# Expert weights loaded four to a DMA instead of two, and earlier in the order of SyncE's queue

## The chip, the cores and the metric

The kernel runs on one core of a Trainium2 chip. The metric is the device time of one execution in microseconds (us), smaller being better. Engines: PE (matrix), DVE (vector), ACT (scalar), POOL (GpSimd), SP (SyncE, which here does nothing but issue DMAs and wait).

## What is computed

Two layers on 16 batches of 128 rows of 256 numbers. Each step adds to x a function of its layer norm:

```
x = x + _L0_xattn_ref(_layernorm(x), k, fside, ctx, ctx, 8)     # long convolution
x = x + _L0_ffn_ref(_layernorm(x), ...)                         # router, top 2 of 16, rank 16
x = x + _L1_xattn_ref(_layernorm(x), ctx, wq, bq, wkv, ...)     # 16-head attention, quantized q and out
x = x + _L1_ffn_ref(_layernorm(x), router_w, ..., gate_w, up_w, down_w, shared_...)

# _L1_ffn_ref
scores = jnp.sqrt(jax.nn.softplus(flat @ router_w.T))
_, idx = jax.lax.top_k(scores + expert_bias, 4)
...
for each of 32 experts: acc + p[:, None] * _clamped_swiglu(flat, wg, wu, wd)
out = out + _clamped_swiglu(flat, shared_gate_w, shared_up_w, shared_down_w)
```

The change concerns the weights of the 32 experts of the last step. One expert has 128 x 768 numbers (gate, up and down), 393 KB; all 32 have 12.6 MB.

## The kernel before

The program is one loop over ticks (`for t in range(TICKS)`), written out once for each engine. A step stands in the engine's instructions at the tick that a table gives it: `T_PE`, `T_DVE`, `T_ACT`, `T_POOL`, `T_SP`. A tick is not a time: it only sets the order in which each engine meets its steps. `at(t, first, every, n)` places n of them, `every` ticks apart. Batch b of the first three steps of the layers is placed 128 ticks after batch b-1. From tick `LOOP` = 3122 on the expert tiles follow: 95 tiles of 128 rows, each with the rows of one expert.

Rows reach their experts through memory. For each batch ACT writes the normed rows four times to `xn_rows` (`Xd`, L1159). SP loads 128 of these rows into one of seven buffers `stage` (`row_load`, L1402; 64 loads, j = 4b + k). POOL scatters them by an indirect DMA to their places in `expert_rows` (`Xs`, L1387). Load j waits until scatter j-7 has completed (`d_sc`), since it takes the same buffer; scatter j waits for load j (`d_st`) and for the routing of its group of batches (`ixl`, which DVE makes at L1007). The groups are batches 0 to 3, 4 to 7, 8 to 11, 12 to 13, 14 to 15. After scatter 55, the last of batch 13, SP gathers the rows of the first tiles (L1455, L1471, `work<-expert_rows`), and PE transposes them (L371) and multiplies (L387, L354). The loads of batches 14 and 15 follow behind the twelfth gather.

The weights of the experts lie in `arena`, 768 columns for each. The same columns serve earlier work: those of experts 0 to 19 (`early` = 20) hold `kv`, `z` and `vT` of the convolution, and so SP waits for `s_uT` and `s_swb`; those of 20 to 27 hold `u` and the transposed context `cT`, and so SP waits for `s_vp`, NB of them (the value projection of the last batch, L493 on PE); those of 28 to 31 hold `xT`, `hb`, `wx` and `kz`, and so SP waits for `s_S` (the scores of the last batch, L630). These are the steps "w0" (L1432), "w1" (L1436) and "w2" (L1440) of SP. PE waits for all of them before its first expert matmul (L381). All DMAs that SP issues go to one hardware queue; ACT's go to another, POOL's to a third.

Other steps that the prediction speaks of: POOL's `rsD` (L1302 to L1306, the reciprocal deviation of the last layer norm, one for each batch), ACT's `xnD` (L1115 at this place, the normed rows), PE's `xnTD` (L536, L537, their transposes), `op` (L529, output projection of attention), ACT's "xr" (L1171, loads of rows for the shared expert) with their transposes on PE (L550), and the shared expert's last matmul `dn` (L570).

Of the kernel before, what the change touches and what calls it, by code (L numbers as in the profile page):

```python
# [15 lines left out]
NE = 32  # L16
# [31 lines left out]
NP = NB // 2  # L48
# [20 lines left out]
def at(t, first, every, n):  # L69
    d = t - first  # L70
    return (d // every,) if d >= 0 and d % every == 0 and d // every < n else ()
# [35 lines left out]
def build(nc, a_x, a_ctxT, a_tk, a_pack, a_qp, a_rows, a_w, a_dest, a_pad, out):  # L107
    ctx = ExitStack()
    with ctx:
# [23 lines left out]
        wv_ = arena[:, :].rearrange("p (e n) -> p e n", n=768)  # L133
        work = sb("work", [128, WORK])

        def cutter(base):
# [22 lines left out]
        early = 20  # L159
# [40 lines left out]
        st = {n: sb(f"st{n}", [128, 2, 16]) for n in "ABCD"}  # L200
# [66 lines left out]
        d_w = sem("d_w")  # L267
# [9 lines left out]
        s_wq, s_wqT, s_wint, s_wsc, s_swb = (sem(n) for n in ("s_wq", "s_wqT", "s_wint", "s_wsc", "s_swb"))  # L277
# [41 lines left out]
            "xnC": 878, "q": 923, "PT": 1035}  # L319
        T_POOL = {"rsA": 131, "rsB": 699, "rsC": 827, "rsD": 1170, "vc": 315, "us": 415, "kv": 296, "xb": 818,  # L320
            "xc": 1118, "list": 1926}
        T_SP = {"fill": 1162, "st": 1863, "w0": 2620, "w1": 3043, "w2": 3053}
        TICKS = LOOP + PACE * (NT + 9)

        def when(table, name, g):
# [9 lines left out]
        def tensor_program(pe):  # L335
# [4 lines left out]
            def tile_steps(t):  # L340
                if t < NT:
                    m = int(t >= EARLY)
                    i, w = t - EARLY * m, (NWE, NWL)[m]
                    field = (words[m][i % w] >> 5 * (i // w)) & 31
                    base[t] = [pe.snap(field * 768, min_val=0, max_val=768 * (NE - 1))]
                for n in at(t, 5, 1, NT):
                    p = ybanks[n % 2]
                    if n >= 2:
                        pe.wait_ge(s_y, n - 1)
                    else:  # L350
                        pe.wait_ge(*sbanks.free[n])
                    pe.wait_ge(s_hT, n + 1)
                    for k, e in enumerate(base.pop(n)):
                        i = pe.matmul(p[U * k:U * k + U, 0:256], hT[n % 2][:, U * k:U * k + U],  # L354
                                      arena[:, 512:][:, bass.ds(e, 256)], start=True, stop=True)
                    i.then_inc(s_yp, 1)
                for n in at(t, 0, 1, NT):
                    p = xbanks[n % 2]
                    if n < 2:
                        pe.wait_ge(*(banks.free[3], cbanks.free[0])[n])  # L360
                    if n == 46:
                        pe.wait_ge(s_tm, 1)
                        pe.transpose(p[0:4, 256:384], th4[:, 0:4], ident).then_inc(s_t5, 1)
                    if n == 48:
                        pe.wait_ge(s_tm, 2)
                    if n == 50:
                        pe.transpose(p[0:1, 256:260], th4[0:4, 4:5], ident[0:4, 0:4]).then_inc(s_t5, 1)
                    if n == 52:
                        pe.wait_ge(s_tm, 3)
                    pe.wait_ge(d_g[n % 4], 16 * Q * (n // 4 + 1))  # L370
                    pe.transpose(p[:, 0:128], xg[n % NX][:, 0:128], ident)  # L371
                    pe.transpose(p[:, 128:256], xg[n % NX][:, 128:256], ident).then_inc(s_gP, 1)
                for n in at(t, 4, 1, NT):
                    if n == 0:
                        pe.wait_ge(s_oT, NB)
                    pe.wait_ge(s_h2, n + 1)
                    pe.transpose(po[:, 0:128], th[n % 3][:, 0, :], ident).then_inc(s_hP, 1)  # L377
                for n in at(t, 1, 1, NT):
                    p = gbanks[n % 2]
                    if n == 0:  # L380
                        pe.wait_ge(d_w, 16 * NE // 2)  # L381
                    if n < 2:
                        pe.wait_ge(*banks.free[n])
                    pe.wait_ge(s_gT, n + 1)
                    for c in range(2):
                        for k, e in enumerate(base[n]):
                            i = pe.matmul(p[U * k:U * k + U, 0:256], xgT[n % 3][:, 128 * c + U * k:128 * c + U * k + U],  # L387
                                          arena[:, 256 * c:][:, bass.ds(e, 256)], start=(c == 0), stop=(c == 1))
                    i.then_inc(s_gup, 1)

            pe.wait_ge(d_id, 16)
            for t in range(TICKS):
# [3 lines left out]
                for n in at(t, T_PE["wsc"], 16, 2):  # L396
                    p, free = bk.take(("wint", n), s_wint, n + 1)
# [4 lines left out]
                    for c in range(2):  # L402
                        for k in range(2):
                            o = 256 * k + 128 * c
                            i = pe.transpose(pb[:, o:o + 128], wtb[:, 256 * c + 128 * k:256 * c + 128 * k + 128], idb[:, :])
# [3 lines left out]
                    p, free = bk.take(("swb", n), s_swb, 1)  # L409
                    pe.wait_ge(*free)  # L410
                    pe.wait_ge(s_pconst, 1)
                    for c in range(2):
                        i = pe.matmul(p[:, 128 * c:128 * c + 128], ones[:, :], wdg[:, c, :], start=True, stop=True)
                    i.then_inc(s_wsc, 1)
                for b in at(t, T_PE["xnTA"], 128, NB):
                    p, free = bk.take(("vT", b), s_vT, b + 1)
# [4 lines left out]
                for n in at(t, T_PE["uT"], 128, 2 * NP):  # L421
                    r, co = n // 2, n % 2
                    p, free = bk.take(("xA", n), s_xA, n + 1)
# [3 lines left out]
                    for half in range(2):  # L427
# [3 lines left out]
                        for k in range(8):  # L431
                            i = pe.matmul(pv, zv[:, k, :], ident, is_transpose=True, start=False, stop=(k == 7))  # L432
                    i.then_inc(s_uT, 1)
                for b in per(t, T_PE["xnTB"]):
                    p, free = bk.take(("xT", b), s_xT, b + 1)
# [4 lines left out]
                for b in per(t, T_PE["h"]):  # L440
                    p, free = bk.take(("h", b), s_eh, b + 1)
# [8 lines left out]
                for b in per(t, T_PE["rl"]):  # L450
                    p, free = bk.take(("l", b), s_l, b + 1)
# [136 lines left out]
                for m in (*at(t, T_PE["wordE"], 1, 1), *(1 for _ in at(t, T_PE["word"], 1, 1))):  # L588
                    n = len(words[m])
# [803 lines left out]
        def sync_program(sp):  # L1393
# [30 lines left out]
            for t in range(TICKS):  # L1424
                for e in (*at(t, 0, 1, 14), *(14 + n for n in at(t, T_SP["fill"], 36, NE - 14))):
                    sp.dma_start(Xs[e * NB * 128:(e + 1) * NB * 128, :].rearrange("(j p) d -> p j d", p=128),
                                 stage[:, e % 4, :].unsqueeze(1).broadcast_to((128, NB, ROW))).then_inc(d_zero, 16)
                for i in at(t, T_SP["w0"], 32, early // 2):
                    if i == 0:
                        sp.wait_ge(s_uT, 2 * NP)  # L1430
                        sp.wait_ge(s_swb, 1)
                    sp.dma_start(wv_[:, 2 * i:2 * i + 2, :], a_w[2 * i:2 * i + 2].rearrange("e p n -> p e n")).then_inc(d_w, 16)  # L1432
                for _ in at(t, T_SP["w1"], 1, 1):
                    sp.wait_ge(s_vp, NB)
                    for e0 in range(early, NE - 4, 2):
                        sp.dma_start(wv_[:, e0:e0 + 2, :], a_w[e0:e0 + 2].rearrange("e p n -> p e n")).then_inc(d_w, 16)  # L1436
                for _ in at(t, T_SP["w2"], 1, 1):
                    sp.wait_ge(s_S, 4 * NB)
                    for e0 in range(NE - 4, NE, 2):
                        sp.dma_start(wv_[:, e0:e0 + 2, :], a_w[e0:e0 + 2].rearrange("e p n -> p e n")).then_inc(d_w, 16)  # L1440
                for g in range(NG - 1):
                    for n in at(t, when(T_SP, "st", g), (16, 16, 8, 8)[g], KT * (GROUPS[g][1] - GROUPS[g][0])):
                        row_load(KT * GROUPS[g][0] + n)
# [125 lines left out]
```

## Time and profile before

| | us |
|---|---|
| three runs | 693.38, 694.88, 698.75 (median 694.88) |
| the profiled execution, its own time | 698.75 |
| its span, first to last instruction | 697.0 |
| PE, DVE, ACT, POOL busy in it | 582.6, 449.2, 385.6, 378.5 |

The profile is of one execution, the slowest of the three; its span leaves 1.75 us of its time outside. A busy time is the sum over an engine's instructions, and tells nothing of what waits for what: for that there are the chain that ended last and the timelines.

### The profile page before, as it was taken

The page shows a single profiled execution, that of the slowest core. Times are in us where ns is not written, and L with a number is a line of the kernel's source. Part 1 is how long each engine was busy: PE and PEld are TensorE (multiplying, and loading weights), DVE is VectorE, ACT ScalarE, POOL GpSimd, SP SyncE. Part 2 cuts the span into 40 slices and gives each one's busy share as a digit, 9 for nine tenths or more (in the row PEclk, how much of TensorE's full clock was granted, in tenths as well). Part 3 has the DMA queues.
Part 4 walks back from the last instruction along what each step waited for, and adds up shares of the span by engine and source line. Part 5 has one row for each costly group of instructions (what it writes and reads, how often), then busy time and mean ns, then how long its engine had stood idle before and what let it go on. Part 6 is the DMA issues. An engine that isn't in the chain of part 4 may idle for free.

```text
span 697.0 us, 14316 instructions
## 1 busy us (share of the span) xinstructions
PE 582.6 (84%) x4069; PEld 467.5 (67%) x4069; DVE 449.2 (64%) x1392; ACT 385.6 (55%) x1132; POOL 378.5 (54%) x527
## 2 busy tenths in 40 slices
PE   1588999999989999989898788785779999999920
PEld 0487787887767778867776566563557787787810
DVE  1546656777766876767666666375756777555596
ACT  1002456666777656875567866663535666566610
POOL 6847847357554565586554415424255555555560
PEclk9999999999999999999999979886899999999975
DMA  7989999999999995212334945849544555455689
GB/s 272 246 180 334 335 334 334 334 328 327 318 305 331 317 307 171 72 62 90 120 114 142 352 132 148 264 131 327 164 141 124 167 161 155 152 160 161 206 271 309
DMA packets 135868, 155.02 MB, mean 222 GB/s; under 512 B 15376, under 2 KB 125072, under 8 KB 135536
## 3 DMA queue, kind: packets, MB, share of 16 engines
q1 hardware_dynamic: 117664, 122.50, 59.2%
q0 software_dynamic: 7632, 20.98, 8.4%
q10 hardware_dynamic: 10496, 10.62, 4.9%
q8 instruction: 36, 0.59, 0.4%
q14 instruction: 40, 0.33, 0.2%
HBM read 53.92 MB, written 100.28 MB: 221 GB/s over the span
## 4 chain that ended last, share of the span: by engine, by line
PE 60%; DVE 12%; POOL 8%; issue 7%; DMA 5%; ACT 5%; ACTq 0%; another core or an unknown queue 0%; SPq 0%; DVEq 0%; POOLq 0%
PE ps L387 11%; PE pc L650 10%; PE pS L354 6%; POOL arena L1373 4%; PE pS L630 4%; PE ps L432 3%; PE po L601 2%; DMA work<-y_rows 2%; PE ps L616 2%; PE ps L459 2%; PE ps L493 2%; DMA expert_rows<-stage,ixl 2%; PE ps L476 2%; PE ps L562 1%; PE ps L485 1%
## 5 line engine op out<-in xcount | busy, mean ns | idle before, releaser
L650 PE MATMUL pc<-arena,tk 128*128 128x128 f32 x768 | 109.7, 296 | 13.3 <-POOL arena L1373 7.3
L650 PEld LDWEIGHTS pc<-arena,tk 128*128 128x128 f32 x768 | 97.9, 204 | 25.7 <-issue 13.5
L1373 POOL TENSOR_TENSOR arena<-arena 128x512 f32<-128x512 f32 x64 | 90.5, 1428 | 20.7 <-ACT arena L1178 20.6
L387 PE MATMUL ps<-arena,work 128*128 x380 | 100.0, 386 | 0.6 <-ACT work L1132 0.6
L1387 POOL DMA_INDIRECT expert_rows<-stage,ixl x64 | 64.0, 1000 | 45.4 <-DVE ixl L1007 22.4
L1245 ACT ACTIVATE work<-pS,work 128x128 f32<-128x128 f32 x256 | 72.7, 369 | 4.9 <-DVE work L909 3.7
L706 DVE TENSOR_SCALAR work<-ps 128x256 f32<-128x256 f32 x95 | 40.1, 422 | 49.9 <-PE ps L387 46.4
L387 PEld LDWEIGHTS ps<-arena,work 128*128 128x128 f32 x380 | 66.0, 194 | 6.5 <-issue 1.2
L354 PE MATMUL pS<-arena,tk 128*128 x190 | 60.7, 401 | 4.7 <-ACT tk L1127 3.4
L1122 ACT ACTIVATE tk<-work 128x128 f32<-128x128 f32 x95 | 29.5, 311 | 63.3 <-DVE work L706 52.3
L909 DVE TENSOR_REDUCE work<-pS 128x4 f32<-128x512 f32 x64 | 43.9, 686 | 27.0 <-PE pS L630 25.4
L891 DVE TENSOR_TENSOR arena<-pc,arena 128x512 f32<-128x512 f32 x64 | 43.5, 679 | 17.8 <-PE pc L650 17.7
L1314 POOL DMA_INDIRECT y_rows<-tk,work x38 | 41.3, 1087 | 24.6 <-ACT tk L1137 19.3
L354 PEld LDWEIGHTS pS<-arena,tk 128*128 128x128 f32 x190 | 28.7, 189 | 22.9 <-issue 15.4
L616 PE MATMUL ps<-pk,work 128*128 128x128 f32 x256 | 40.5, 282 | 3.0 <-ACT work L1245 1.8
L1237 ACT ACTIVATE work<-ps 128x512 f32<-128x512 f32 x64 | 37.9, 592 | 3.0 <-PE ps L616 0.8
L630 PE MATMUL pS<-arena,work 32*128 32x256 f32 x256 | 38.1, 417 | 0.8 <-ACT work L1230 0.8
L1302 POOL TENSOR_TENSOR stB<-stB,epsc 128x1 f32<-128x1 f32 x16 | 3.0, 190 | 62.2 <-DVE stB L666 62.0
L1302 POOL TENSOR_TENSOR stD<-stD,epsc 128x1 f32<-128x1 f32 x16 | 3.2, 200 | 60.3 <-DVE stD L666 60.0
L616 PEld LDWEIGHTS ps<-pk,work 128*128 128x128 f32 x256 | 29.7, 143 | 6.8 <-issue 3.3
L432 PE MATMUL ps<-pk,arena 128*128 128x128 f32 x256 | 32.3, 273 | 0.0
L1127 ACT ACTIVATE tk<-po 128x128 f32<-128x128 f32 x95 | 25.9, 272 | 9.7 <-PE po L377 5.8
(286 smaller groups left out, 1444.8 us busy)
## 6 DMA issues: line engine op xcount, KB each, us to landing
expert_rows<-stage SPq DMA_DIRECT2D x32, 2080.0 KB, 21.4
work<-expert_rows SPq DMA_DIRECT2D x95, 130.0 KB
arena<-in_w SPq DMA_DIRECT2D x16, 768.0 KB
stage<-xn_rows SPq DMA_DIRECT2D x64, 130.0 KB
xn_rows<-xnD ACTq DMA_DIRECT2D x16, 512.0 KB
work<-y_rows SPq DMA_DIRECT2D x16, 512.0 KB
tk<-in_tk SPq DMA_DIRECT2D x1, 2048.0 KB, 9.6
out<-xs SPq DMA_DIRECT2D x16, 128.0 KB, 3.1
```

The costliest lines, as they stand in the source:

```text
L354: i = pe.matmul(p[U * k:U * k + U, 0:256], hT[n % 2][:, U * k:U * k + U], arena[:, 512:][:, bass.ds(e, 256)], start=True, stop=True)
L387: i = pe.matmul(p[U * k:U * k + U, 0:256], xgT[n % 3][:, 128 * c + U * k:128 * c + U * k + U], arena[:, 256 * c:][:, bass.ds(e, 256)], sta ...
L432: i = pe.matmul(pv, zv[:, k, :], ident, is_transpose=True, start=False, stop=(k == 7))
L616: i = pe.transpose(p[:, 128 * k:128 * k + 128], Pt[m % 3][:, 128 * k:128 * k + 128], ident)
L630: i = pe.matmul(p[:, 256 * c:256 * c + 256], qT[b % 3][r, 128 * c:128 * c + 128], kz[b % 3][r, c, :, :].rearrange("p a b -> p (a b)"), sta ...
L650: i = pe.matmul(pv, tk[:, h, 128 * d:128 * d + 128], kvv[:, ci, :, :].rearrange("p b (i h j) -> p (b i) h j", i=8, h=8)[:, :, hl, :], star ...
L891: dve.tensor_tensor(zv, cbanks.place["conv", n][:, :].rearrange("p (k h j) -> p k h j", h=4, j=8), x1, ALU.mult).then_inc(s_z, 1)
L909: dve.tensor_reduce(mx[:, g, :], sbanks.place["S", m][:, :].rearrange("p (k m) -> p k m", k=4), AX.X, ALU.max, negate=True).then_inc(s_mx, 1)
L1245: i = act.activation(Pt[m % 3][:, 128 * k:128 * k + 128], sbanks.place["S", m][:, 128 * k:128 * k + 128], ACT.Exp, bias=mx[:, g, k:k + 1])
L1314: pool.indirect_dma_start(out=Yr, out_offset=bass.IndirectOffsetOnAxis(ap=xg[n % NX][:, 256:257].bitcast(U32), axis=0), in_=y[n % NY], in_ ...
L1373: pool.tensor_tensor(kv[kk % 4][:, c, half, :].rearrange("p (i h j) -> p i h j", h=8, i=8), i0, i1, ALU.mult).then_inc(s_kv, 1)
L1387: pool.indirect_dma_start(out=Xs, out_offset=bass.IndirectOffsetOnAxis(ap=ixl[:, b, k:k + 1], axis=0), in_=stage[:, j % NS, :], in_offset= ...
```

## The change

Every weight DMA carries four experts (1536 KB) instead of two (768 KB), so that there are 8 in place of 16. PE's wait counts 8 in place of 16. The ten DMAs of w0, placed 32 ticks apart from tick 2620 on, become five that all stand at tick 2620. w1 moves from tick 3043 to 2878, and w2 from 3053 to 3034. The waits ahead of w0, w1 and w2 stay as they are. Bytes and their places are the same.

```diff
-        T_SP = {"fill": 1162, "st": 1863, "w0": 2620, "w1": 3043, "w2": 3053}
+        T_SP = {"fill": 1162, "st": 1863, "w0": 2620, "w1": 2878, "w2": 3034}
...
                     if n == 0:
-                        pe.wait_ge(d_w, 16 * NE // 2)
+                        pe.wait_ge(d_w, 16 * NE // 4)
...
-                for i in at(t, T_SP["w0"], 32, early // 2):
-                    if i == 0:
-                        sp.wait_ge(s_uT, 2 * NP)
-                        sp.wait_ge(s_swb, 1)
-                    sp.dma_start(wv_[:, 2 * i:2 * i + 2, :], a_w[2 * i:2 * i + 2].rearrange("e p n -> p e n")).then_inc(d_w, 16)
+                for _ in at(t, T_SP["w0"], 1, 1):
+                    sp.wait_ge(s_uT, 2 * NP)
+                    sp.wait_ge(s_swb, 1)
+                    for e0 in range(0, early, 4):
+                        sp.dma_start(wv_[:, e0:e0 + 4, :], a_w[e0:e0 + 4].rearrange("e p n -> p e n")).then_inc(d_w, 16)
                 for _ in at(t, T_SP["w1"], 1, 1):
                     sp.wait_ge(s_vp, NB)
-                    for e0 in range(early, NE - 4, 2):
-                        sp.dma_start(wv_[:, e0:e0 + 2, :], a_w[e0:e0 + 2].rearrange("e p n -> p e n")).then_inc(d_w, 16)
+                    for e0 in range(early, NE - 4, 4):
+                        sp.dma_start(wv_[:, e0:e0 + 4, :], a_w[e0:e0 + 4].rearrange("e p n -> p e n")).then_inc(d_w, 16)
                 for _ in at(t, T_SP["w2"], 1, 1):
                     sp.wait_ge(s_S, 4 * NB)
-                    for e0 in range(NE - 4, NE, 2):
-                        sp.dma_start(wv_[:, e0:e0 + 2, :], a_w[e0:e0 + 2].rearrange("e p n -> p e n")).then_inc(d_w, 16)
+                    for e0 in range(NE - 4, NE, 4):
+                        sp.dma_start(wv_[:, e0:e0 + 4, :], a_w[e0:e0 + 4].rearrange("e p n -> p e n")).then_inc(d_w, 16)
```

The instructions of PE, DVE, ACT and POOL stand in the same order as before. SP's do not. Its DMAs from w0 to w2 before, `stage<-xn_rows` being row loads and the row load behind the first five weight DMAs being load 32:

```order
L1432 DMA arena<-in_w 128x2x768 x5
L1402 DMA stage<-xn_rows 128x260
L1432 DMA arena<-in_w 128x2x768
L1402 DMA stage<-xn_rows 128x260 x4
L1432 DMA arena<-in_w 128x2x768
L1402 DMA stage<-xn_rows 128x260 x4
L1432 DMA arena<-in_w 128x2x768
L1402 DMA stage<-xn_rows 128x260 x4
L1432 DMA arena<-in_w 128x2x768
L1402 DMA stage<-xn_rows 128x260 x3
L1432 DMA arena<-in_w 128x2x768
L1402 DMA stage<-xn_rows 128x260 x7
```

The same place of SP in the changed kernel, from the row loads ahead of w0 to the register load behind w2:

```order
L1402 DMA stage<-xn_rows 128x260 x32
L1432 DMA arena<-in_w 128x4x768 x5
L1402 DMA stage<-xn_rows 128x260 x13
L1436 DMA arena<-in_w 128x4x768 x2
L1402 DMA stage<-xn_rows 128x260 x8
L1440 DMA arena<-in_w 128x4x768
L1402 DMA stage<-xn_rows 128x260 x3
L1452 TENSOR_LOAD tk
```

The five loose DMAs of w0 between row loads 32 and 48 are gone; w1 stands 10 row loads earlier, between 44 and 45, and w2 three earlier, between 52 and 53.

What SP waits for at the end of the row loads before (rows 52 to 55, with w1 and w2 around the last of them):

```order
L1402 DMA stage<-xn_rows 128x260 [waits d_sc3,d_xn1]
L1402 DMA stage<-xn_rows 128x260 [waits d_sc4]
L1402 DMA stage<-xn_rows 128x260 [waits d_sc5]
L1436 DMA arena<-in_w 128x2x768 [waits s_vp]
L1436 DMA arena<-in_w 128x2x768 x3
L1402 DMA stage<-xn_rows 128x260 [waits d_sc6]
L1440 DMA arena<-in_w 128x2x768 [waits s_S]
```

What SP waits for around w1 in the changed kernel (row loads 43 and 44 ahead of it, 45 to 48 behind):

```order
L1402 DMA stage<-xn_rows 128x260 [waits d_sc1]
L1402 DMA stage<-xn_rows 128x260 [waits d_sc2,d_xn1]
L1436 DMA arena<-in_w 128x4x768 [waits s_vp]
L1436 DMA arena<-in_w 128x4x768
L1402 DMA stage<-xn_rows 128x260 [waits d_sc3]
L1402 DMA stage<-xn_rows 128x260 [waits d_sc4]
L1402 DMA stage<-xn_rows 128x260 [waits d_sc5]
L1402 DMA stage<-xn_rows 128x260 [waits d_sc6,d_xn0]
```

Row loads 45 to 48 now stand behind the wait for `s_vp`, which only w1, the last row load of batch 13 and w2 stood behind before.

## Rows read from the trace of the kernel before

**Rows 1.** Busy us by stretch: engines, then PE's granted clock, DMA share, GB/s

```profile
480.00:490.00 10.00, 4.26 (x14) 2.27 (x12) 2.94 (x11) 4.14 (x11) 2.32 (x4) 0.50 0.74 224
550.00:580.00 30.00, 30.00 (x164) 24.02 (x163) 22.82 (x83) 19.25 (x74) 17.27 (x19) 1.00 0.55 161
```

**Rows 2.** The chain that ended last, 466 to 489 us: start, us, what

```profile
467.79 6.04 DMA expert_rows<-stage,ixl
...
473.85 5.54 DMA stage<-xn_rows
...
480.16 4.74 DMA expert_rows<-stage,ixl
...
485.15 3.47 DMA work<-expert_rows
```

**Rows 3.** Timeline of SP: start, duration, line, DMA, count merged

```profile
379.58 2.87 SPq L1432 DMA_DIRECT2D arena<-in_w  x5
...
442.57 2.14 SPq L1402 DMA_DIRECT2D stage<-xn_rows  x3
444.75 0.49 SPq L1432 DMA_DIRECT2D arena<-in_w  x1
...
466.38 2.21 SPq L1436 DMA_DIRECT2D arena<-in_w  x4
...
474.23 0.98 SPq L1440 DMA_DIRECT2D arena<-in_w  x2
```

**Rows 4.** Timeline of SP, 465 to 466.4 us: row load 54

```profile
466.01 0.32 SPq L1402 DMA_DIRECT2D stage<-xn_rows  x1
```

**Rows 5.** Timeline of PE, in brackets its idle us before, and for whom

```profile
445.86 1.91 PE L493 MATMUL ps<-pk,arena 128*128 128x256 f32 x4
...
463.20 0.42 PE L536 MATMUL ps<-pk,xnD 128*128 128x128 f32 x1
...
468.87 0.27 PE L550 MATMUL ps<-pk,tk 128*128 128x128 f32 x1
...
478.80 0.58 PE L529 MATMUL ps<-wint,work 128*128 128x256 bf16 x2 [0.62 <-ACT work L1257]
...
485.66 1.20 PE L570 MATMUL ps<-tk 128*128 128x256 f32 x2
488.76 0.45 PE L371 MATMUL ps<-pk,work 128*128 128x128 f32 x1 [1.90 <-DMA work<-expert_rows]
```

**Rows 6.** Timeline of POOL: scatters 32, 44, 45, rsD, 47, 48, 54, 55, rsD

```profile
422.27 1.06 POOL L1387 DMA_INDIRECT expert_rows<-stage,ixl  x1 [0.43 <-issue]
...
443.00 0.96 POOL L1387 DMA_INDIRECT expert_rows<-stage,ixl  x1 [0.30 <-issue]
446.79 0.96 POOL L1387 DMA_INDIRECT expert_rows<-stage,ixl  x1 [2.83 <-DMA stage<-xn_rows]
...
459.49 0.19 POOL L1302 TENSOR_TENSOR stD<-stD,epsc 128x1 f32<-128x1 f32 x1 [10.47 <-DVE stD L666]
...
461.20 1.07 POOL L1387 DMA_INDIRECT expert_rows<-stage,ixl  x1 [0.30 <-issue]
467.79 0.96 POOL L1387 DMA_INDIRECT expert_rows<-stage,ixl  x1 [5.53 <-DVE ixl L1007]
...
476.05 0.96 POOL L1387 DMA_INDIRECT expert_rows<-stage,ixl  x1 [0.30 <-issue]
480.16 1.12 POOL L1387 DMA_INDIRECT expert_rows<-stage,ixl  x1 [3.15 <-DMA stage<-xn_rows]
481.29 0.37 POOL L1302 TENSOR_TENSOR stD<-stD,epsc 128x1 f32<-128x1 f32 x1
```

**Rows 7.** Timeline of ACT, 452 to 462 us

```profile
453.14 0.39 ACTq L1171 DMA_DIRECT2D tk<-xn_rows  x1
...
461.01 0.60 ACT L1115 ACTIVATE xnD<-xs,stD 128x256 f32<-128x256 f32 x1 [2.35 <-POOL stD L1306]
```

**Rows 8.** GB/s moved, 444 to 484 us, in 40 slices of 1 us

```profile
GB/s 217 269 173 280 317 343 400 136 61 31 264 233 25 0 0 0 0 0 139 330 187 9 6 207 255 421 366 359 419 423 408 419 421 398 410 397 411 386 329 29
```

## The prediction, made before the changed kernel was run

> **What bounds the kernel now.** I read the stretches first, then the chain that ended last, then the timelines of the engines that it passes through. In the expert loop PE is the bound: between 550 and 580 us it is busy for all of 30.00 us at the full granted clock [rows 1]. So time gained or lost ahead of the loop goes on to the end one for one, and a DMA can matter only through what starts the loop. Just ahead of it, from 480 to 490 us, PE is busy for only 4.26 of 10 us, at a granted clock of 0.50 (the lower level, 1.2 GHz) [rows 1]: here PE waits. The chain says for what. It runs through DMAs alone: scatter 48 (6.04 us), row load 55 into the buffer that it frees (5.54), scatter 55 (4.74), and the gather of the first tile's rows (3.47) [rows 2]. The gather lands at 485.15 + 3.47 = 488.62, and PE's first transpose of the loop begins at 488.76 after 1.90 us of idling for it [rows 5]. The work of PE that stands ahead ends at 485.66 + 1.20 = 486.86 [rows 5]. The weights are nowhere in the chain. What they do is fill the DMA engines just then: w1 is issued at 466.38, w2 at 474.23 [rows 3], and from 469 to 482 us some 400 GB/s are moved, as much as the trace shows anywhere near [rows 8].
>
> **What the change can give.** w1 waits for `s_vp`, which is complete when L493 ends, at 445.86 + 1.91 = 447.8 [rows 5]. Before, it was issued 18.6 us later, because it stood behind the loads of batch 13. Now it goes out at 447.9, into a stretch in which the DMA engines stand nearly still from 456 to 462 [rows 8]. The chain's DMAs are then free of it. The nearest unloaded prices: scatter 47 started at 461.20 and released the load into its buffer at 466.01, 4.8 us [rows 6, 4]; a transfer of the same 130 KB took 3.47 us as the gather [rows 2]. POOL issues the eight scatters of batches 12 and 13 in order; from 48 to 54 that takes 476.05 - 467.79 = 8.26 us [rows 6], so 55 can follow 1.3 us later, 9.5 us behind 48. Its load is not later than that: 4.8 + 3.5 = 8.3 us behind 48, and 0.8 us more from landing to scatter (479.39 to 480.16 [rows 2, 6]). So with scatter 48 where it was, scatter 55 starts at 477.3 in place of 480.16, completes at 482.1, and the gather, issued 0.26 us later as now, lands at 485.8 in place of 488.62. That is 2.8 us earlier. But PE is busy till 486.86. What is late next is the attention of batch 15, through `op` (478.80), `rsD` and the shared expert's L570 [rows 5, 6]. The most that this part gives is 1.9 us.
>
> **What it costs.** SP is one queue. Row loads 45, 46 and 47, issued from 442.57 on before [rows 3], now stand behind the wait for L493 and behind the 3.15 MB of w1. Startup and issue take about 1.2 us (issued at 466.38, the slices of 467 and 468 move 207 and 255, that of 469 moves 421 [rows 3, 8]); 3.15 MB at 0.40 MB/us are 7.9 us [rows 8]; ACT's load of 0.26 MB at 453.14 [rows 7] shares the engines, 0.6 us at most; the row's own 0.13 MB and its landing 0.3 to 1.7 us. From 447.9 that puts load 45 down at 458.0 to 459.3. Before it landed just ahead of 446.79 [rows 6]. Scatter 45 follows 0.8 us later, 46 1.3 us behind that, and 1.0 us later the next in POOL's order: `rsD` of batch 14, which ran at 459.49 as soon as DVE had its input [rows 6]. Now it begins at 461.1 to 462.4, 1.6 to 2.9 us late. ACT's L1115 waits for it (461.01 before, 2.35 us of idle [rows 7]), and PE's L536 for that. L1115 ended at 461.61, and PE came to L536 at 463.20 [rows 5, 7]: a cover of 1.6 us. What is left is 0 to 1.3 us, which shifts PE, and with it the attention of batch 15, the routing `ixl` of group 12 to 13, and the scatters from 48 on. I take 0.9, in the upper half, since ACT's work behind L1115 has less cover than PE.
>
> **The other parts.** w2 now stands behind load 52, which waits for scatter 45: 459.5 + 4.8 = 464.3 at the earliest, 465.5 at the latest. Its 1.57 MB take 4 us, so it is done by 470.5, ahead of load 55's release at 473. Loads 53 and 54, behind it in the queue, land by 472 and are due from 474 on; this is covered by some 2 us. w0 issues 7.86 MB in one piece at 379.58 instead of 3.93 MB there [rows 3] and the rest in five pieces up to 444.75. At 0.40 MB/us the queue is full until about 400, or 405 with the traffic of the others; row load 32 lies behind it. Scatter 32 ran at 422.27 [rows 6], so 17 us of cover hide it; without that cover it would cost the 2.4 MB added there, 6 us. The pieces taken away at 390 to 444.75 stood beside row loads that had slack, except the last, issued right ahead of load 48 [rows 3], whose scatter came only at 467.79; they give nothing. Half as many issues: the four of w1 took 2.21 us of SP [rows 3]; two larger ones cost between half of that and all of it, a gain of 0 to 1.1 us on a queue that then waits for other things. ACT's load at 453.14 now shares the engines with w1, but its transposes came at 468.87 [rows 7, 5]: 12 us of cover even if it took 3.5 us more. PE's wait for the weights ends at about 470, far ahead of its first expert matmul.
>
> **The sum.** The gather is ready at 485.8 + 0.9 = 486.7; PE is free at 486.86 + 0.9 = 487.8. The first transpose moves from 488.76 to 487.8: a gain of 1.0 us. The profiled execution took 698.75 (span 697.0, 1.75 outside); it would take 697.7. Against the median, which is 3.9 us below the profiled one, I forecast 694.88 - 1.0 = 693.9 us.
>
> **Where a page is weighed against the rows.** The Trainium skill, "DMA: Bandwidth & Descriptors", section "Rules for kernel authors", asks for at least 1 MiB a DMA, and its section "Bandwidth" has 341 GB/s at 1 MB and 425 at 16 MB. In this trace 768 KB DMAs, issued back to back, already go with their neighbours at 386 to 423 GB/s from 472 to 482 us [rows 8]. By the page w1 would be some per cent shorter, an estimate of 0.4 us from its two figures, and the sum 1.4 instead of 1.0; by the rows there is nothing to gain from size. I go by the rows. A second fork is the order within a queue. Load 55, issued behind w1, took 5.54 us against the 3.47 of the gather [rows 2], which it would also do if all shared alike. The same page, section "Queues, rings and completion order", says that an engine consumes the descriptors of a ring in order. By that rule load 45 waits for all of w1; if it does not hold, load 45 lands 3.5 us after its issue, at 452.6, POOL is never held, and the gain is the whole 1.9.
>
> **Rivals.** (1) *The held POOL queue costs more than the freed chain gives.* If w1 runs at the 224 GB/s that the stretch 480 to 490 had [rows 1] in place of 400, it takes 14.0 instead of 7.9 us; load 45 lands at 465, `rsD` of batch 14 starts 9 us late, and after 1.6 us of cover 7.4 us remain: 1.9 - 7.4 = 5.5 us slower, 700.4. It decides for slower once load 45 lands after about 460.0 (3.5 us of delay against 1.6 of cover and 1.9 of gain). For it: SP's queue has everything behind one wait. Against: w1 alone fills 448 to 457, with next to no other traffic, and the rate near 400 held for 13 us. A moderate form, load 45 at 461 to 462, gives 695.9 to 696.9. (2) *Load 45 is not held.* w1 goes faster or the load passes it: 1.9 us, 693.0. (3) *The granted clock moves.* It is 0.50 from 480 to 490 [rows 1], after PE had idled. If less idling keeps it at the upper level through that stretch, the 4.26 us of PE's work take half, and the attention chain gives up to 2 us more; the gather then binds at 486.7. Together 2.1 us there and up to 1 in the first tiles: 691.8. The same may go the other way elsewhere, 2 us. (4) *Nothing changes,* since the loop's start is set by something that I have as covered: 694.9.
>
> **How the numbers follow.** The forecast has 0.45; rival 2 0.12; 3 0.11; 4 0.14; rival 1 0.18, nearly all in its moderate form. Three runs of before lie between 693.38 and 698.75, so a median of few moves by 2 us by itself; 1% is 6.9 us, about what a measurement of this kernel tells from no change. The range reaches from 690.5, rival 3 with a good draw of runs, to 698.0, rival 1 in its moderate form with a poor one. A gain beyond 1% would need 6.9 us, more than all of PE's idling between 471 and 489 that a DMA is part of: 0.04. A loss beyond 1% takes rival 1 in full and more: 0.06. Within 1%: 0.90.
>
> **What would show it.** In the changed profile: w1 issued near 448 and w2 near 465; POOL idle from 444 to about 459 for `stage<-xn_rows`, and `rsD` of batch 14 at 461 to 462; POOL's scatters 48 to 55 at an even 1.3 us with no wait before 55; the gather landing ahead of PE's last L570; and PE's first L371 released by PE's own work or ACT's, not by a DMA. I am wrong if POOL's wait ends much before 456 or after 461, if w0's burst delays scatter 32 or a step of attention, or if the start of the loop is the same and the time moves by the clock alone.

## The result

The changed kernel takes 700.75 us (median of 5 runs, 698.94 to 701.64) against 694.88 for the kernel before (693.38 to 698.75, by then 5 runs as well). The ratio is 1.0064, 95% interval 1.0034 to 1.0094: 4.4 us slower, where 1.0 us faster was forecast. The ratio is not the quotient of the two medians, here or below: the medians of the five lie 5.9 us apart, while the mean of all 14 runs kept of the changed kernel, 700.0, lies 4.6 us above the mean of the five before, 695.5. The loss is under 1%, but it is clear of the noise, and the time lies above the end of the range (698.0). The profiled execution has a span of 699.9 us (its time 701.65) against 697.0.

The queue of SP in the changed kernel (its timeline: start, duration, line, DMA, count) answers to [rows 3]:

```profile
442.16 0.94 SPq L1436 DMA_DIRECT2D arena<-in_w  x2
443.14 14.77 SPq L1402 DMA_DIRECT2D stage<-xn_rows  x8
457.96 0.43 SPq L1440 DMA_DIRECT2D arena<-in_w  x1
...
480.95 9.32 SPq L1471 DMA_DIRECT2D work<-expert_rows  x12
```

and the longest wait of SP from 440 to 485 us (for what, us in total, times, the longest):

```profile
SPq L1436 <- PE ps L493: 14.1, 1, 14.1
```

w1 goes out with the end of L493, as meant, and the row loads 45 to 52 follow it. What they meant for the others shows in the chain that ended last (start, us, what):

```profile
442.59 0.51 SPq L1436
...
443.14 10.82 DMA stage<-xn_rows
...
457.00 0.21 POOL stD L1302
...
458.33 0.61 ACT xnD L1115
...
459.07 0.45 PE ps L536
...
472.13 4.00 another core or an unknown queue
```

Before, the chain ran through row loads and scatters from 468 on [rows 2]. Now it goes from L493 through the issue of w1: row load 45 is issued at 443.14 and lands 10.8 us later, POOL comes to `rsD` of batch 14 at 457.00, and ACT and PE wait for that. The timelines of POOL and of PE, against [rows 6] and [rows 5]:

```profile
454.73 0.98 POOL L1387 DMA_INDIRECT expert_rows<-stage,ixl  x1 [15.38 <-DMA stage<-xn_rows]
456.02 0.96 POOL L1387 DMA_INDIRECT expert_rows<-stage,ixl  x1 [0.31 <-issue]
457.00 0.20 POOL L1302 TENSOR_TENSOR stD<-stD,epsc 128x1 f32<-128x1 f32 x1
...
473.87 0.96 POOL L1387 DMA_INDIRECT expert_rows<-stage,ixl  x1 [0.30 <-issue]
...
440.38 1.74 PE L493 MATMUL ps<-pk,arena 128*128 128x256 f32 x4
...
454.07 1.16 PE L562 MATMUL ps<-tk 128*128 128x128 f32 x8
459.07 0.45 PE L536 MATMUL ps<-pk,xnD 128*128 128x128 f32 x1 [3.84 <-ACT xnD L1115]
...
463.69 2.03 PE L562 MATMUL ps<-tk 128*128 128x128 f32 x8
...
476.74 2.05 PE L562 MATMUL ps<-tk 128*128 128x128 f32 x8 [4.34 <-ACT tk L1267]
...
487.76 0.42 PE L371 MATMUL ps<-pk,work 128*128 128x128 f32 x1
```

POOL waits 15.38 us for load 45 (2.83 before). PE idles for 3.84 us before L536 of batch 14, where it did not idle before. The eight matmuls L562 take 1.16 us before that idle time and 2.03 behind it: PE has run part of this stretch at 1.2 instead of 2.4 GHz. The view by windows has it in the granted clock, the third number from the end (ahead of the DMA share and GB/s). The kernel before has a slow stretch of the kind too, with 0.74 from 460 to 470 us, but there it lies ahead of L536:

```profile
450.00:460.00 10.00, 4.78 (x40) 3.25 (x36) 5.65 (x23) 4.02 (x10) 4.04 (x6) 0.94 0.78 249
460.00:470.00 10.00, 8.81 (x64) 6.89 (x56) 6.08 (x28) 4.89 (x15) 4.71 (x5) 0.71 0.86 293
```

The side that was meant to gain does gain: scatter 55 follows its neighbours at 473.87 without a wait (3.15 us before), and no DMA releases PE's first L371. That L371 starts at 487.76, 1.0 us earlier than before, just what I forecast, and by luck: this execution had come to the end of L493 at 442.1 and that of before at 447.8, so from there to the loop the changed kernel took 45.6 us against 41.0.

Nor does the first transpose L371 decide when the expert matmuls begin. The first of them, L387, waits for ACT's L1132, the copies of the transposed rows. PE in the changed kernel, then before:

```profile
490.25 2.07 PE L387 MATMUL ps<-arena,work 128*128 x4 [1.42 <-ACT work L1132]
...
490.19 2.07 PE L387 MATMUL ps<-arena,work 128*128 x4 [0.34 <-ACT work L1132]
```

With the gather in time, ACT is what is late: its routing steps of the last group of batches (L1281 to L1288, with 1.28 us of loading a table) stand ahead of its L1132. L387 starts 2.3 us behind the end of PE's work ahead of the loop (L570), where it was 3.3 us before. So of the 1.9 us that PE idled for the gather only 1.0 could be won.

Two of the waits in this stretch are of another kind. Nothing that the profile knows releases them. Here are ACT's and DVE's, and the matmuls whose result DVE's L928 takes:

```profile
476.22 0.38 ACT L1267 ACTIVATE tk<-ps 128x256 f32<-128x256 f32 x1 [4.09 <-remote]
...
440.26 0.42 DVE L928 TENSOR_SCALAR tk<-ps 128x256 f32<-128x256 f32 x1 [4.65 <-remote]
...
437.40 1.13 PE L562 MATMUL ps<-tk 128*128 128x128 f32 x8 [3.30 <-ACT tk L1267]
```

I call them stray waits. ACT's 4.09 us stand in the chain, and account for most of the 4.6 us by which the loop starts later than before in these two profiles. Of DVE's 4.65 us only the last 1.7 are stray, from the end of L562 at 438.53 to 440.26: an idle time of about this length belongs to this place. The kernel before has 3.82 us there, put down to "issue", and its L928 starts with the end of L562. The stray waits had to be told from the change's own cost.

### The profile page after: what moved, and what is told of

Its sections match the earlier page's. It is cut to its first block, busy times and chain, and to the rows that moved or that the text cites. A ratio compares the mean times of both kernels' runs of the same rounds, so it can differ in the third digit from the quotient of the medians.

```text
span 699.9 us, 14308 instructions
## 1 busy us (share of the span) xinstructions
PE 581.5 (83%) x4069; PEld 468.0 (67%) x4069; DVE 448.3 (64%) x1392; ACT 385.2 (55%) x1132; POOL 377.6 (54%) x527
## 4 chain that ended last, share of the span: by engine, by line
PE 65%; DVE 10%; POOL 8%; ACT 6%; issue 6%; DMA 4%; another core or an unknown queue 1%; SPq 0%; ACTq 0%; DVEq 0%; POOLq 0%
PE ps L387 12%; PE pc L650 10%; PE pS L354 6%; POOL arena L1373 4%; PE pS L630 4%; PE ps L432 3%; PE ps L616 3%; DMA work<-y_rows 2%; PE po L601 2%; PE ps L562 2%; PE ps L493 2%; PE ps L472 2%; PE po L377 2%; PE ps L476 2%; DMA stage<-xn_rows 2%
## 5 line engine op out<-in xcount | busy, mean ns | idle before, releaser
L650 PE MATMUL pc<-arena,tk 128*128 128x128 f32 x768 | 108.3, 294 | 13.3 <-POOL arena L1373 7.3
L387 PE MATMUL ps<-arena,work 128*128 x380 | 102.1, 393 | 1.4 <-ACT work L1132 1.4
L387 PEld LDWEIGHTS ps<-arena,work 128*128 128x128 f32 x380 | 67.2, 197 | 7.4 <-issue 1.8
L1314 POOL DMA_INDIRECT y_rows<-tk,work x38 | 41.2, 1084 | 25.6 <-ACT tk L1137 22.7
L630 PE MATMUL pS<-arena,work 32*128 32x256 f32 x256 | 36.2, 400 | 0.8 <-ACT work L1230 0.8
L1127 ACT ACTIVATE tk<-po 128x128 f32<-128x128 f32 x95 | 25.9, 273 | 12.3 <-PE po L377 9.8
```

The costliest lines, as they stand in the source:

```text
L630: i = pe.matmul(p[:, 256 * c:256 * c + 256], qT[b % 3][r, 128 * c:128 * c + 128], kz[b % 3][r, c, :, :].rearrange("p a b -> p (a b)"), sta ...
L650: i = pe.matmul(pv, tk[:, h, 128 * d:128 * d + 128], kvv[:, ci, :, :].rearrange("p b (i h j) -> p (b i) h j", i=8, h=8)[:, :, hl, :], star ...
L1314: pool.indirect_dma_start(out=Yr, out_offset=bass.IndirectOffsetOnAxis(ap=xg[n % NX][:, 256:257].bitcast(U32), axis=0), in_=y[n % NY], in_ ...
```

## The experiments

There are four sets of runs, each on a chip of its own with the kernel before beside it. The sets differ: the kernel before took 684.3, 684.5 and 685.7 us in the first, third and fourth, 696.2 in the second, where the profiles have stray waits; in the others no profile has one over 1 us. So only times within a set are compared.

What I read in every profile is counted from the end of the last L493 (the value projection of batch 15), since `s_vp` is complete then: the start of scatter 45, the start of `rsD` of batch 14, PE's idle time before its L536, and the start of the loop (the first L371). They are read from the timelines of POOL and PE. Each row has one profile, that is one execution. The start of the loop spreads by 3 us between executions of like kernels (37.1 to 40.1 with w1 behind load 47, without stray waits), so the ratios, from many runs, decide.

| kernel | w1 | scatter 45 | rsD | PE idle | loop | ratio, interval |
|---|---|---|---|---|---|---|
| before | behind 54 | -1.0 | 11.7 | 0 | 41.0 | 1 |
| changed | ahead of 45 | 12.6 | 14.9 | 3.84 | 45.6 | 1.0064, 1.0034 to 1.0094 |
| e0_again | ahead of 45 | 12.3 | 14.5 | 2.47 | 41.7 | 1.0042, 1.0024 to 1.0060 |
| e0_third | ahead of 45 | 13.2 | 15.4 | 4.38 | 42.4 | 1.0034, 1.0014 to 1.0054 |
| e1_ticks | ahead of 45 | 12.0 | 14.3 | 3.25 | 39.5 | 1.0031, 1.0010 to 1.0052 |
| e2_burst | behind 54 | -2.4 | 11.7 | 0 | 39.8 | 0.9998, 0.9976 to 1.0020 |
| e3_behind47 | behind 47 | 0.6 | 11.7 | 0 | 38.3 | 0.9982, 0.9959 to 1.0005 |
| e3_again | behind 47 | 0.3 | 11.5 | 0.65 | 37.3 | 0.9989, 0.9965 to 1.0014 |
| e3_third | behind 47 | 0.0 | 11.5 | 0.65 | 37.3 | 0.9954, 0.9928 to 0.9979 |
| e4_wait_only | behind 47, wait ahead of 45 | 2.8 | 11.5 | 0.65 | 35.0 | 0.9977, 0.9955 to 0.9999 |
| e5_half | half and half | 7.6 | 11.6 | 0.78 | 37.6 | 0.9970, 0.9950 to 0.9991 |
| e5_again | half and half | 7.8 | 11.6 | 0.64 | 37.2 | 0.9981, 0.9956 to 1.0006 |
| e6_act_queue | on ACT's queue | 3.0 | 11.6 | 0.72 | 38.0 | 0.9957, 0.9934 to 0.9980 |
| e7_behind47_by4 | behind 47 | -2.1 | 16.1 | 0 | 43.2 | 1.0100, 1.0075 to 1.0126 |
| e7_again | behind 47 | -1.4 | 11.7 | 0 | 37.1 | 0.9978, 0.9950 to 1.0005 |
| e7_third | behind 47 | -2.6 | 11.7 | 0 | 40.1 | 0.9962, 0.9939 to 0.9985 |
| e8_by4_spread | behind 47 | 0.6 | 11.7 | 0 | 37.1 | 0.9972, 0.9945 to 0.9999 |
| e9_by2_burst | behind 47 | -1.5 | 11.7 | 0 | 38.8 | 0.9984, 0.9956 to 1.0013 |

### The change again, and its two halves (first set)

**e0_again** is the changed kernel unedited.

> The changed kernel once more, as the anchor of this call and for a second profile. Held queue (theory A: w1 stands ahead of row loads 45 to 47, so POOL waits for load 45 until some 12 us after L493 ends, rsD of batch 14 comes late and PE idles for it): 3 to 6 us slower than the kernel before, and the profile has a wait of POOL for stage<-xn_rows of over 12 us and an idle time of PE before L536 of 2 to 4 us. Burst (theory B: the 7.9 MB of w0 in one piece slow the engines from 380 to 410 us): as slow, but with the loss between 380 and 420 us. Stray (theory C: the waits of 2 to 4 us on something unnamed in ACT and DVE, seen once at 472 us, are the loss): as slow only if they are there again at the same place.

Measured: 687.63 us against 684.26, 1.0042. The stray waits are gone on this chip and the loss is there, with a wait of 14.04 us of POOL and 2.47 us of PE. Its timelines of POOL and PE:

```profile
451.29 0.96 POOL L1387 DMA_INDIRECT expert_rows<-stage,ixl  x1 [14.04 <-DMA stage<-xn_rows]
...
455.61 0.45 PE L536 MATMUL ps<-pk,xnD 128*128 128x128 f32 x1 [2.47 <-ACT xnD L1115]
```

**e1_ticks**: the kernel before, with only the two places changed.

```diff
-"w0": 2620, "w1": 3043, "w2": 3053
+"w0": 2620, "w1": 2878, "w2": 3034
```

> The kernel before with only the two places changed (w1 at tick 2878, w2 at 3034); two experts to a DMA, w0 spread as before. A, held queue: all of the loss is here, 3 to 6 us slower than before, POOL waits over 10 us for load 45. B, burst: no slower than before (within 1 us). C, stray: no slower, or by chance.

Measured: 687.31 against 684.26, 1.0031. PE idles again, in the timeline of PE:

```profile
460.02 0.30 PE L536 MATMUL ps<-pk,xnD 128*128 128x128 f32 x1 [3.25 <-ACT xnD L1115]
```

**e2_burst**: the changed kernel with the two places put back.

```diff
-"w0": 2620, "w1": 2878, "w2": 3034
+"w0": 2620, "w1": 3043, "w2": 3053
```

> The changed kernel with w1 and w2 put back to ticks 3043 and 3053: four experts to a DMA and w0 in one burst remain. A, held queue: as the kernel before, within 1.5 us. B, burst: 3 to 6 us slower, like the changed kernel.

Measured: 684.62 against 684.26, 0.9998 (0.9976 to 1.0020). POOL's `rsD` waits for DVE and for no DMA:

```profile
451.95 0.19 POOL L1302 TENSOR_TENSOR stD<-stD,epsc 128x1 f32<-128x1 f32 x1 [11.84 <-DVE stD L666]
```

The places carry the loss; four experts to a DMA and the burst of w0 carry none that can be measured.

**e3_behind47**: the kernel before with w1 early, but behind row load 47.

```diff
-"w0": 2620, "w1": 3043, "w2": 3053
+"w0": 2620, "w1": 2910, "w2": 3034
```

> The kernel before with w1 at tick 2910 (behind row load 47 and the last DMA of w0, ahead of row load 48) and w2 at 3034. The weights are as early as in the change, but no row load that POOL needs before rsD of batch 14 stands behind them. A: not slower than before, 0 to 2 us faster, since the chain through load 55 is free of weights; POOL waits under 4 us for load 45. B: as before. If this is 3 us slower too, it is not the held POOL queue but early weights as such (their traffic at 448 to 462 us).

Measured: 683.14 against 684.26, 0.9982. w1 went out with the end of L493 (at 440.43), as in e0_again (at 439.06), so its bytes were as early; what differs is what stood behind them. POOL's `rsD` is on time, and PE begins its loop with no DMA to wait for:

```profile
452.11 0.19 POOL L1302 TENSOR_TENSOR stD<-stD,epsc 128x1 f32<-128x1 f32 x1 [8.89 <-DVE stD L666]
...
454.38 0.44 PE L536 MATMUL ps<-pk,xnD 128*128 128x128 f32 x1
...
478.75 0.42 PE L371 MATMUL ps<-pk,work 128*128 128x128 f32 x1
```

So early weights are not the cost; the three row loads behind them are. w2 stands at 3034 here too, so it is not the cost either: between e1_ticks and e3_behind47 only w1's place differs, 2878 against 2910, and the times are 4.2 us apart.

### What holds load 45: the wait, the bytes, or the queue (second set)

**e4_wait_only**: as e3, with SP's wait for `s_vp` alone put ahead of load 45.

```diff
+                for _ in at(t, 2878, 1, 1):
+                    sp.wait_ge(s_vp, NB)
                 for _ in at(t, T_SP["w1"], 1, 1):
```

> SP waits for s_vp where the change has w1 (ahead of row load 45), but the DMAs of w1 go out behind row load 47; w2 at 3034; two experts to a DMA. It takes the wait without the bytes. If the wait alone is the cost (rival): POOL waits for load 45 until 10 us or more after L493 ends, and it is 2 to 4 us slower than with w1 wholly behind load 47. If the bytes ahead in the queue are the cost (my theory): load 45 is issued with the end of L493 and lands 3 to 4 us later, rsD of batch 14 is not late (within 12 us of the end of L493), PE does not idle before L536, and the time is within 1 us of the kernel before or up to 2 us under it.

Measured: 694.06 against 696.2, 0.9977. Scatter 45 starts 2.8 us behind the end of L493, `rsD` is not late. The wait alone costs nothing that shows.

**e5_half**: the changed kernel with half of w1 behind load 47.

```diff
-                    for e0 in range(early, NE - 4, 4):
+                    for e0 in range(early, early + 4, 4):
...
+                for _ in at(t, 2910, 1, 1):
+                    for e0 in range(early + 4, NE - 4, 4):
```

> The changed kernel with half of w1 (four experts, 1.57 MB) ahead of row load 45 and half behind row load 47. My theory (bytes in the queue, with a threshold at the moment at which DVE has the input of rsD, 11.7 us after the end of L493): load 45 lands some 4 us earlier than with all of w1 ahead, so scatter 45 starts 8 to 9 us after the end of L493 and rsD of batch 14 is not late; no idling of PE before L536; time within 1 us of the kernel before. A rival in which the loss goes in proportion to the bytes ahead: half the loss, 1.5 us slower than before, with PE idling 1 to 2 us before L536.

Measured: 694.61 against 696.2, 0.9970. Scatter 45 starts at 7.6 us, between 2.8 (no bytes ahead) and 12.6 (all of them), and nothing of it reaches `rsD`: half the bytes cost nothing that shows. The rows of POOL:

```profile
451.98 0.96 POOL L1387 DMA_INDIRECT expert_rows<-stage,ixl  x1 [10.41 <-DMA stage<-xn_rows]
...
456.00 0.18 POOL L1302 TENSOR_TENSOR stD<-stD,epsc 128x1 f32<-128x1 f32 x1 [1.79 <-DVE stD L666]
```

POOL waited 10.41 us for the load and then still 1.79 us for DVE. That 1.79 is what was left of POOL's cover; the other half of w1, some 5 us more, goes beyond it.

**e6_act_queue**: the changed kernel with w1 issued by ACT.

```diff
+                for _ in at(t, 2914, 1, 1):
+                    act.wait_ge(s_vp, NB)
+                    for e0 in range(early, NE - 4, 4):
+                        act.dma_start(wv_[:, e0:e0 + 4, :], a_w[e0:e0 + 4].rearrange("e p n -> p e n")).then_inc(d_w, 16)
...
                     sp.wait_ge(s_vp, NB)
-                    for e0 in range(early, NE - 4, 4):
-                        sp.dma_start(wv_[:, e0:e0 + 4, :], a_w[e0:e0 + 4].rearrange("e p n -> p e n")).then_inc(d_w, 16)
```

> The changed kernel with the two DMAs of w1 issued by ACT, on its own queue, at the moment at which they went out on SP's; SP keeps its wait for s_vp ahead of row load 45. Bytes in flight, their time and the moment at which load 45 is issued are as in the change; only the order within one queue is gone. If load 45 was late because it stood behind w1 in the same queue: it now lands 3 to 6 us after its issue, and POOL is free by 8 us after the end of L493. If it was late because w1 fills the DMA engines, whatever the queue: 9 to 11 us after its issue as in the change, and as slow as the change.

Measured: 694.3 against 696.2, 0.9957. ACT issues w1 and SP issues load 45 at the same moment; in the timelines of ACT, SP and POOL:

```profile
444.61 0.99 ACTq L1164 DMA_DIRECT2D arena<-in_w  x2
...
444.61 1.88 SPq L1406 DMA_DIRECT2D stage<-xn_rows  x4
...
447.53 0.96 POOL L1391 DMA_INDIRECT expert_rows<-stage,ixl  x1 [5.73 <-DMA stage<-xn_rows]
452.23 0.96 POOL L1391 DMA_INDIRECT expert_rows<-stage,ixl  x1 [3.74 <-DMA stage<-xn_rows]
456.14 0.19 POOL L1306 TENSOR_TENSOR stD<-stD,epsc 128x1 f32<-128x1 f32 x1 [2.95 <-DVE stD L666]
```

Scatter 45 starts 2.9 us after the issue of its load, against 11.6 in the changed kernel, with the same 3.15 MB in flight. With e4 and e5 this makes the order within SP's queue the mechanism. One thing is not separated: load 45 was issued together with w1 here, not 1 us behind it. But load 46, issued at 444.98 and so behind the first of w1's DMAs, was scattered 7.7 us after L493 against 13.9 in the changed kernel. Sharing is not free either: load 46 came in at about 451.5, 6 us or more behind its issue. That agrees with the Trainium skill, "DMA: Bandwidth & Descriptors", section "Queues, rings and completion order", by which a DMA engine takes the descriptors of one ring in their order and goes round between the rings of different queues. Whether a load that is issued on the other queue well into w1's transfer would be as quick was not tried.

**e7_behind47_by4**: the changed kernel with w1 behind load 47.

```diff
-"w1": 2878, "w2": 3034
+"w1": 2910, "w2": 3034
```

> The changed kernel with one number changed: w1 at tick 2910 instead of 2878, behind row load 47 instead of ahead of 45. Four experts to a DMA, w0 in one burst, w2 at 3034 as in the change. My theory: all of the loss is gone; 0 to 2 us faster than the kernel before. If burst and size had a cost that only shows with early weights: 1 us or more slower than with two experts to a DMA in the same places.

Measured: 704.06 against 696.2, 1.0100: a miss. Scatter 45 was early and load 45 did nothing to `rsD`, but `rsD` was late all the same, for DVE. The timelines of ACT, DVE and PE have the reason, a stray wait on ACT ahead of a step for which PE waits, and then PE at the lower clock (L630 took 1.13 us in e5_half, L562 1.16):

```profile
446.04 0.31 ACT L1272 ACTIVATE tk<-tk 128x128 f32<-128x128 f32 x1 [2.86 <-remote]
...
443.03 0.42 DVE L928 TENSOR_SCALAR tk<-ps 128x256 f32<-128x256 f32 x1 [4.68 <-remote]
...
447.10 0.66 PE L616 MATMUL ps<-pk,work 128*128 128x128 f32 x4 [2.02 <-ACT work L1230]
447.69 1.85 PE L630 MATMUL pS<-arena,work 32*128 32x256 f32 x8
449.47 2.08 PE L562 MATMUL ps<-tk 128*128 128x128 f32 x8
```

w1 was issued at 446.10, behind ACT's wait, so its traffic is not what ACT waited for. SP was late as well: w1 was due with the end of L493 at 444.87, and ACT, DVE (its L940) and SP all go on between 446.04 and 446.10. This is one profile; that it is the reason for all six runs (700.1 to 705.2) fits, but is not shown.

### Size and spread with w1 early (third set)

e7_again and e3_again are the two kernels above; the other two fill the square of size and spread.

> The kernel with w1 at 2910, four experts to a DMA and w0 in one burst, once more, because it was 1.0% slower than before where I had expected 0 to 2 us faster. Its profile had waits on something unnamed of 4.7 us (DVE L928) and, new, 2.9 us (ACT L1272), after which PE ran at the granted clock of 0.50. Theory C (these waits are the chip's or the draw's, not the kernel's): now within 2 us of the kernel before, or faster, and on a chip that shows no such waits up to 2 us faster. Theory S (size or burst of w0 costs once w1 is early): again 4 us or more slower, on any chip.

> w1 at 2910, w2 at 3034, two experts to a DMA, w0 spread, once more: 0 to 2 us faster than before by the held-queue theory on any chip. If it is 4 us or more slower here, early weights do not pay on such a chip and the first result was that chip's.

**e8_by4_spread**, from e7:

```diff
-                for _ in at(t, T_SP["w0"], 1, 1):
+                for i in at(t, T_SP["w0"], 64, early // 4):
```

> As the kernel of e7, but w0 spread over the same ticks as before (five DMAs, 64 ticks apart). Between the two: if it is as slow as e7, four experts to a DMA are the cost; if it is as fast as e3, the burst is. Theory C: all four of this call within 2 us of each other.

**e9_by2_burst**, from e3:

```diff
-                for i in at(t, T_SP["w0"], 32, early // 2):
+                for i in (range(early // 2) if t == T_SP["w0"] else ()):
```

> As e3, but all ten DMAs of w0 at tick 2620, two experts each: the burst alone. As slow as e7 if the burst is the cost; as fast as e3 if it is the size. Theory C: within 2 us of the others.

Measured, against 684.52: e7_again 683.78, e3_again 683.58, e8 682.49, e9 683.55. All four within 1.3 us of each other and 0.7 to 2.0 under the kernel before. Neither size nor spread costs or gives anything that shows on this chip (the intervals reach some 2 us either way), and e7's 1.0% is not there.

### Once more (fourth set)

> The changed kernel again. Held queue: 2 to 5 us slower than the kernel before on any chip. Where the chip shows the unnamed waits of ACT and DVE, up to 2 us more or less than that.

> w1 at 2910 with four experts to a DMA and w0 in one burst, for the third time. If this call's chip shows the unnamed waits (kernel before at some 695 us): 1.0% slower again would say that this kernel, with these waits, loses each time; within 2 us would say that it was the draw. On a chip without them (before at some 684 us): 0 to 2 us faster, as in the call before, and the question stays open.

> w1 at 2910, w2 at 3034, two experts to a DMA, w0 spread, for the third time: 0 to 2 us faster than before on any chip by the held-queue theory; on a chip with the unnamed waits it has not run yet.

> The changed kernel with half of w1 ahead of row load 45 and half behind 47, once more: by the threshold theory 0 to 2 us faster than before; by a loss in proportion to the bytes ahead 1 to 2 us slower.

Measured, against 685.65: e0_third 687.49 (1.0034), e7_third 683.33 (0.9962), e3_third 682.67 (0.9954), e5_again 682.89 (0.9981). The changed kernel is slower for the third time, the three that keep all or most of w1 away from the row loads are faster, e7 and e3 with intervals wholly below 1. This chip has no stray waits either, so whether e7 loses each time on one that has them stays open.

## Why the prediction was wrong, step by step

- **What bounds the start of the loop: right in kind; the gain of 1.9 us: too high.** With w1 early and the row loads free, scatters 48 to 55 run evenly and no DMA releases the first L371; in e2_burst, with w1 where it was, PE still idles 0.92 us for the gather. But I counted to L371, and behind it L387 waits for ACT's L1132. From the end of PE's L570 to L387 it was 3.3 us before, 2.3 in e2_burst and 2.3 to 2.4 with w1 early: a gain of 1.0 us in the profile that I read and next to none in e2's. The times with w1 wholly behind load 47 on the quicker chips are 0.11 to 0.46% under the kernel before in five comparisons of e3 and e7, 0.7 to 3.0 us, in two of them clear of the noise. Where more than 1 us of it comes from is open.
- **The landing of load 45: right in kind, a little short.** I had 10.2 to 11.5 us from the end of L493, though my own terms begin at 9.5 (447.9 + 1.2 + 7.9 + 0.3, with nothing for ACT's load); it took 11.8 (443.14 + 10.82, from 442.1). `rsD` was then 2.6 to 3.7 us late (14.3 to 15.4 against 11.7), against 1.6 to 2.9.
- **The cover of 1.6 us: this step failed.** I read it as the time from the end of ACT's L1115 (461.61) to PE's coming to L536 (463.20 [rows 5, 7]), and took it to be the kernel's. It was that execution's. PE ran L562 just ahead of L536 at the lower clock (2.08 us) and came to L536 15.4 us after L493. e2_burst and e7_third, at the lower clock there too, have the same 15.4. Where L562 ran wholly at the full clock (1.16 us), as in the changed kernel, e0_third and e1_ticks, PE was ready for L536 after 13.1 us, and where the clock fell within it (1.94 us in e0_again), after 14.1. ACT's L1115 with a punctual `rsD` ends at 13.6 to 13.8. So there is next to no cover, 0.3 us at most, and in e3_again PE idles 0.65 us even with `rsD` on time. With `rsD` late PE idled 2.5 to 4.4 us, where I had 0 to 1.3.
- **The clock behind the idle time: missing in the forecast, and its cause not shown.** I used the clock for a rival on the fast side only. In all four profiles with PE idle for a late `rsD`, the next L562 took 1.78 to 2.03 us in place of 1.13. But e3_behind47, e7_third and e9_by2_burst, with no idle time at L536, have 1.45 to 1.53 there. With both together, that L562 ended 22.7 to 24.0 us after L493 in these four, against 20.3 in e2_burst and in the kernel before, and 18.0 to 20.1 (once 21.5) with w1 behind load 47 and no stray wait.
- **The sum.** Two pairs differ in nothing but w1's place: e1_ticks against e3_behind47, and e0_third against e7_third. Both are 4.2 us apart: that is the price of the three row loads, where I had 0.9. The kernels with w1 behind load 47 are 0.7 to 3.0 us under the kernel before, so that 1.8 to 3.4 us remain as the loss against it on these chips. Rival 1 in its moderate form, 1 to 2 us slower, was nearest, and had 0.18.
- **The point from which rival 1 decides.** I put it at a landing 12.2 us after L493, with the cover counted in. Measured, 11.8 is already slow, and half of w1 (scatter 45 at 7.6 to 7.8) is not. Where it lies between was not measured. An estimate: scatter 45 starts 2.3 us ahead of `rsD` when POOL has been held (454.73 and 457.00), and DVE has the input of `rsD` for a start at 11.7 us after L493, so scatter 45 must start by about 9.4.
- **w0's burst, the size of the DMAs, w2, the shared expert's rows: right.** e2, and the square of the third set, show nothing. My time for w2 (464.3 to 465.5) did not follow from my own times for scatter 45, which give 463.6 to 464.9; nothing hung on it. No gain came from DMAs of 1,536 KB over 768 KB. The Trainium skill, "DMA: Bandwidth & Descriptors", section "Rules for kernel authors", asks for at least 1 MiB a DMA; these runs show nothing of it.
- **On the first chip** the loss was 4.4 us, more than the 1.8 to 3.4 elsewhere. Its profile has a stray wait of 4.09 us in the chain. Whether that is in most of its runs was not tried, and the halves of the change were not run there. The difference is within what the intervals allow.

The better version is e3 or e7: w1 at tick 2910. On the chips without stray waits e3 was 0.46, 0.18 and 0.11% faster than before, and e7 0.38 and 0.22%. In the one set with stray waits e7 was 1.0% slower and e3 was not run; e4, e5 and e6, whose w1 holds up no row load by much, were 0.2 to 0.4% faster there.

## What to carry to other kernels

A large transfer put early in a queue is paid by what stands behind it in the same queue, and through that by whoever waits in order on another engine: follow it until an instruction that is already late. Place it behind the last small transfer with a reader due soon, or on another queue. And before a gap in a timeline is taken for cover, see at which clock the engine ran up to it: slack of 1.6 us at the lower clock was none at the full one.

## What was not expected of the hardware

- One and the same kernel took 684.3 to 685.7 us in three sets of runs and 694.9 and 696.2 in two, each set on one chip. Some 5 to 10 us of this lie behind the start of the loop (202 to 204 us from the first L371 to the end, against 208 to 213).
- The slower ones have waits of ACT and DVE that no instruction or DMA in the profile releases, of up to 4.7 us, in varied number; one of 1.7 to 1.8 us ahead of ACT's L1209 is in all six profiles. At DVE's L928 near 440 us the wait of 4.6 to 4.7 us is mostly an ordinary one: on the quicker chips DVE waits 3.0 to 3.9 us there for PE's L562 and starts as it ends; in five of the six slower profiles (not in that of the kernel before) it starts 1.3 to 1.7 us later. The faster ones have none over 1 us on ACT or DVE. What they are was not found out. One ahead of a step that PE needs may cost more than its own length, by the clock: e7_behind47_by4 reads so, in one profile.
